# Fourier channel mixing rewritten: four images in a row, columns held twice, each layer as four 64x64 parts of the array

## The chip, the cores and the metric

The kernel runs on one core of a Trainium2 chip. The metric is the device time of one execution in microseconds (us), the median of the runs. The core has five engines with a queue each: TensorE (PE; its weight loads are listed apart as PEld), VectorE (DVE), ScalarE (ACT), GpSimd (POOL) and SyncE (SP). A suffix q (SPq, ACTq) is an engine's sequencer, which issues DMAs, waits and branches.

## The reference, cut to what matters

The model is a chain of attention, Fourier mixing, attention, routed experts and retention on an input of 4 images, 48x48 tokens, 192 channels. The stage at hand is in the second block:

```python
def _L1_conv_ref(x, w1, b1, w2, b2, Wb, bb):
    bias = x @ Wb.T + bb
    xb = x.reshape(Bsz, Hh, Ww, nb, bs)                       # 4 blocks of 48 channels
    xf = jnp.fft.rfftn(xb, axes=(1, 2), norm='ortho')
    y = jnp.einsum('bhwnd,ndk->bhwnk', xf, w1) + b1           # complex, block by block
    y = _crelu(y)                                             # relu of the real and the imaginary part
    y = jnp.einsum('bhwnd,ndk->bhwnk', y, w2) + b2
    out = jnp.fft.irfftn(y, s=(Hh, Ww), axes=(1, 2), norm='ortho')
    return out.reshape(Bsz, Hh, Ww, Cc) + bias
```

The two-dimensional transform is split: `fourier_front` does the rows (48 positions to 25 complex values), `fourier_mix` the columns, both complex layers and the columns back, `fourier_back` the rows back. `fourier_mix` is what changes. The experts (`run_experts`) compute `gelu(x @ w1 + b1) @ w2 + b2` for 8 experts.

## The kernel before

All stages stand one behind the other in one program. Each allocates its tiles and semaphores, opens a block with one hand-written queue per engine, and ends with a barrier of all engines. Nothing of a stage starts before that barrier, so a stage's length adds to the total as a whole. No scheduler orders anything: each queue runs in the order of the code, and semaphores counted (`full`: a bank is written; `free`: a bank is evacuated) tie them.

`fourier_mix` works on one image at a time, in a hardware loop (`Fori`, a counted loop with a branch back at its end) over the 4 images on SP, PE and ACT. An image is 48 rows, real and imaginary (96 partitions), by 25 columns by 192 channels in float32. The channels are handled as two halves of 96 (two blocks of 48 each).

1. SP (L1031) loads the image into the one tile `columns`, two DMAs of 900 KB. It waits for `full` at the image's first use number (L1029), that is until PE has done everything of the image before.
2. PE (L1052) transforms the columns: 5 matmuls of 96 columns each fill a PSUM bank (one of four accumulators of 512 float32 per partition), 10 banks in all. ACT copies each into `layer0` (L1100).
3. PE does the two layers (L1064, L1066, L1068): for each of 10 groups per layer one matmul with the real weights over 480 columns and two with the imaginary ones (one negated) over 240 columns. The weights are 96x96 with two 48x48 blocks on the diagonal and zeros elsewhere. ACT evacuates each bank in two pieces with the bias, and in the first layer relu (L1109).
4. PE transposes the result, 50 transposes in 13 banks (L1076); ACT copies them into `turned` (L1116).
5. PE transforms back, 10 matmuls of 480 columns (L1083); ACT copies into `back` (L1123) and issues two DMAs of 900 KB to `mixed` (L1127).

PE takes a bank when the use four before it is evacuated (`take`, L1043). VectorE only negates the weights once (L1091). A float32 matmul shows as two records of PEld and two of PE in the trace, a transpose as one.

`run_experts` runs its 8 experts two to a pass of a loop that is opened by `hinted` (L29), which marks the branch back for the instruction fetch on each engine (L2188, L2219, L2231).

## Time and profile before

| what | us |
|---|---|
| median of 3 runs | 7612.12 |
| the runs | 7607.83 to 7624.61 |
| profiled execution, own time | 7621.83 |
| profiled execution, span | 7620.3 |
| `fourier_mix`, first matmul to last copy | 2758.02 to 3030.56 |
| PE busy in the span | 6538.7 (86%) |
| mean granted TensorE clock | 0.904 |

The profile gives for each stretch the busy time of every engine, the clock that TensorE was granted (1.00 is its 2.4 GHz level, 0.50 its 1.2 GHz level) and what the DMA engines moved. The timeline gives instructions in order of time, equal ones merged: the start, the time covered, the engine, the line, the operation, what is written and read, the size of the array part used (rows*columns), shape, count, and the idle time before with what ended it. A matmul's record is longer than the array is occupied by it, since records overlap; so the pace is read from the distance between starts.

### The profile page before, as it was taken

To read this page: it belongs to the slowest core of one execution; us is meant where nothing else is said; L and a number is where in the kernel's file an instruction comes from. 1 tells how busy PE (TensorE), PEld (TensorE's weight loads), DVE (VectorE), ACT (ScalarE), POOL (GpSimd) and SP (SyncE) were. 2 spreads that over 40 slices of the span, in tenths; PEclk is the share of its full clock that TensorE was granted. 3 is DMA by queue.
4 is the path that set the end of the run, shared out by engine and by line. 5 is a ranking of instruction groups with operands and counts; after the bars stand their busy time and mean duration, and the time that the engine had idled before them with its cause. 6 is when DMAs were issued, how large, how long until landed. Compare 5 with 4: busy or idle time off the path is not lost. (4 is left out here: it accounts for less than half of the span.)

```text
span 7620.3 us, 232590 instructions
## 1 busy us (share of the span) xinstructions
PE 6538.7 (86%) x87259; PEld 4110.7 (54%) x87259; DVE 4712.1 (62%) x7690; ACT 3159.9 (41%) x5333; POOL 2306.5 (30%) x2558
## 2 busy tenths in 40 slices
PE   6699999999997677499999995299779999999977
PEld 4255555555554554266767674176445555555546
DVE  6788888888884410222323236211779999999976
ACT  2067666766665134022222221021444444444432
POOL 0011111111111000000000000300349999999961
PEclk8699999999998688699999995599889999999986
DMA  3211111111112422401010003222741111111123
GB/s 117 77 36 38 36 38 34 38 37 38 38 38 56 136 68 53 142 1 29 1 29 1 19 14 118 69 68 49 225 146 36 37 38 36 37 38 36 37 69 100
DMA packets 424933, 428.90 MB, mean 56 GB/s; under 512 B 77729, under 2 KB 397961, under 8 KB 419051
## 3 DMA queue, kind: packets, MB, share of 16 engines
q1 hardware_dynamic: 342123, 339.77, 16.0%
q0 software_dynamic: 62528, 59.16, 3.3%
q10 hardware_dynamic: 19712, 21.53, 0.9%
q8 instruction: 460, 7.54, 0.4%
q14 instruction: 110, 0.90, 0.0%
HBM read 253.62 MB, written 166.55 MB: 55 GB/s over the span
## 5 line engine op out<-in xcount | busy, mean ns | idle before, releaser
L633 DVE TENSOR_REDUCE softmax_part_max<-softmax_ring 128x1 f32<-128x512 f32 (+1 forms) x2880 | 1680.5, 633 | 333.8 <-PE softmax_ring L541 276.4
L2517 POOL TENSOR_TENSOR retention_decayed<-retention_third,retention_decay_table 128x384 f32<-128x384 f32 x1728 | 1690.6, 1005 | 104.3 <-ACT retention_third L2539 100.0
L2498 DVE TENSOR_TENSOR retention_decayed<-retention_scores,retention_decay_table 128x768 f32<-128x768 f32 x1728 | 1654.7, 958 | 90.4 <-PE retention_scores L2459 58.3
L673 ACT ACTIVATE softmax_probs<-softmax_scores 128x768 f32<-128x768 f32 x1728 | 1392.1, 810 | 678.8 <-PE softmax_scores L563 605.8
L541 PE MATMUL softmax_ring<-softmax_k_next,softmax_q_next 96*32 96x512 bf16 (+1 forms) x11520 | 1116.9, 377 | 182.8 <-issue 74.6
L2459 PE MATMUL retention_scores<-retention_q_half,retention_k_piece 96*32 96x384 bf16 x20736 | 1184.7, 325 | 36.1 <-DMA retention_v_piece<-ret_v 29.1
L2539 ACT COPY retention_third<-retention_scores 128x384 f32<-128x384 f32 x1728 | 826.6, 478 | 892.4 <-PE retention_scores L2459 892.4
L2471 PE MATMUL retention_sums<-retention_decayed,retention_v_piece 128*32 128x288 f32 x13824 | 1182.5, 407 | 3.4 <-POOL retention_decayed L2517 0.6
L2459 PEld LDWEIGHTS retention_scores<-retention_q_half,retention_k_piece 96*32 96x32 bf16 x20736 | 625.5, 95 | 520.1 <-DVE retention_decayed L2498 41.7
L574 PE MATMUL softmax_sums<-softmax_probs,softmax_v_piece 128*32 128x192 f32 x13824 | 883.4, 330 | 13.3 <-issue 12.6
L563 PE MATMUL softmax_scores<-softmax_q_third,softmax_k_piece 99*32 99x384 bf16 x13824 | 886.7, 332 | 3.1 <-DMA softmax_v_piece<-rope_v 1.8
L505 POOL DMA_DIRECT2D rope_out<-softmax_result x384 | 195.4, 510 | 1727.1 <-ACT softmax_result L662 1676.0
L541 PEld LDWEIGHTS softmax_ring<-softmax_k_next,softmax_q_next 96*32 96x32 bf16 x11520 | 306.9, 95 | 681.1 <-DVE softmax_part_max L633 437.5
L574 PEld LDWEIGHTS softmax_sums<-softmax_probs,softmax_v_piece 128*32 128x32 f32 x13824 | 425.3, 112 | 208.9 <-issue 29.0
L1493 DVE TENSOR_REDUCE wide_top<-wide_scores 128x1 f32<-128x2304 f32 x72 | 184.1, 2558 | 504.8 <-PE wide_scores L1387 504.8
L2471 PEld LDWEIGHTS retention_sums<-retention_decayed,retention_v_piece 128*32 128x32 f32 x13824 | 344.0, 109 | 260.5 <-issue 179.7
L563 PEld LDWEIGHTS softmax_scores<-softmax_q_third,softmax_k_piece 99*32 99x32 bf16 x13824 | 363.1, 97 | 178.4 <-ACT softmax_probs L673 25.8
L1417 PE MATMUL wide_valued_bank<-wide_v,wide_probs_t 128*128 128x192 f32 x2592 | 440.5, 329 | 2.2 <-ACT wide_probs_t L1481 2.2
L1417 PEld LDWEIGHTS wide_valued_bank<-wide_v,wide_probs_t 128*128 128x128 f32 x2592 | 419.2, 190 | 25.6 <-issue 22.5
L1354 POOL TENSOR_TENSOR wide_residual<-wide_residual,wide_bo 96x2304 f32<-96x2304 f32 x8 | 40.2, 5043 | 1056.2 <-DMA wide_residual<-x 1056.2
L1381 PE MATMUL wide_scores<-wide_qk_t 128*128 128x512 f32 (+1 forms) x720 | 329.4, 559 | 2.3 <-ACT wide_v L1465 2.3
L1472 ACT ACTIVATE wide_probs<-wide_scores,wide_shift 128x2304 f32<-128x2304 f32 x72 | 157.0, 2180 | 414.5 <-DVE wide_shift L1495 414.5
(303 smaller groups left out, 6685.6 us busy)
## 6 DMA issues: line engine op xcount, KB each, us to landing
ret_v<-ret_proj_values SPq DMA_DIRECT2D x8, 1728.0 KB, 8.7
retention_v_piece<-ret_v SPq DMA_DIRECT2D x144, 96.0 KB
softmax_q_third<-rope_q SPq DMA_DIRECT2D x192, 54.0 KB
softmax_q_next<-rope_q POOLq DMA_DIRECT2D x64, 162.0 KB, 3.9
softmax_k_piece<-rope_k SPq DMA_DIRECT2D x192, 54.0 KB
softmax_k_next<-rope_k POOLq DMA_DIRECT2D x64, 162.0 KB, 6.2
ret_q<-ret_proj_parts SPq DMA_DIRECT2D x48, 216.0 KB, 2.8
ret_k<-ret_proj_parts SPq DMA_DIRECT2D x48, 216.0 KB, 3.1
```

What stands on the lines that cost most here:

```text
L541: last = nc.tensor.matmul(ring[m % 2][32 * g:32 * g + 32, 0:width], q_next[i][:, rows:rows + 32], k_next[i][:, at:at + width], start=True, ...
L563: last = nc.tensor.matmul(scores[n % 2][32 * g:32 * g + 32, c, 0:QC], k_piece[t // PT][:, at:at + 32], q_third[third][:, c * QC:(c + 1) * ...
L574: last = nc.tensor.matmul(sums[third % 2][32 * g:32 * g + 32, 0:VC], v_piece[t // PT][:, t % PT, :], probs[n % 4][:, g * VC:(g + 1) * VC], ...
L633: nc.vector.reduce_max(part_max[:, j, c:c + 1], ring[m % 2][:, 0:CHUNKS[c][1]], axis=X)\
L673: nc.scalar.activation(probs[n % 4][:, :].rearrange("p (c q) -> p c q", c=2), scores[n % 2][:, :, 0:QC], ACT.Exp, scale=scale).then_inc(ex ...
L1381: nc.tensor.matmul(scores[:, at:at + width], qk_t[:, 0, 0, i * P:(i + 1) * P], qk_t[:, 1, 0, at:at + width], start=True, stop=False)
L1417: last = nc.tensor.matmul(valued_bank[:, 0:C], probs_t[:, t * P:(t + 1) * P], v[:, t, :], start=(t == 0), stop=(t == TILES - 1))
L2459: last = nc.tensor.matmul(scores[n % 2][32 * g:32 * g + 32, c, 0:QC], k_piece[t // PT][:, at:at + 32], q_half[half][:, c * QC:(c + 1) * QC ...
L2471: last = nc.tensor.matmul(sums[half][32 * g:32 * g + 32, 0:VC], v_piece[t // PT][:, t % PT, :], weights[n % 4][:, g * VC:(g + 1) * VC], st ...
L2498: nc.vector.tensor_tensor(weights[n % 4][:, 0:2 * QC].rearrange("p (c q) -> p c q", c=2), scores[n % 2][:, 0:2, 0:QC], table[:, table_at(n ...
L2517: nc.gpsimd.tensor_tensor(weights[n % 4][:, 2 * QC:HALF], third[n % 3][:, :], table[:, at:at + QC], ALU.mult)\
L2539: nc.scalar.copy(third[n % 3][:, :], scores[n % 2][:, 2, 0:QC]).then_inc(third_copied, 1)
```

## The change

`fourier_mix` is written anew.

- The loop over the images is written out on PE, ACT and DVE (no branch). `columns` exists twice; SP loads images 0 and 1 ahead, image 0 before the tables, and image b+2 as soon as the column transform of image b is issued (`FIRST_LAYER` uses).
- All 8 PSUM banks are used instead of 4. Bank uses are numbered through; even ones are evacuated by ACT (`act_free`), odd ones by DVE (`dve_free`).
- The two 48-channel blocks of a half stand at partitions 0 to 47 and 64 to 111 (`ROW` = 64). A column-transform matmul makes 48 output rows instead of 96, so there are 100 in place of 50 per image.
- A layer handles 10, 10 and 5 values of k at a time, real results in one bank and imaginary ones in another. Each matmul is one block, 48 by 64: (rows 0, columns 0), (64, 64) for the real part and (0, 64), (64, 0) for the imaginary one. The imaginary result thus comes out with its blocks exchanged, and DVE writes them back exchanged (L1172). Eight matmuls of 480 columns serve a group of 10.
- Transposes take 112 columns in place of 96; gaps of 16 are skipped when they are copied. The partitions between the blocks and the weights' borders are cleared by POOL once.
- `hinted` goes, and the loops of `run_experts` become plain `Fori`.

```diff
-def hinted(nc, eng, start, end):
-
-    return nc.Fori(start, end, engines=bass.OrderedEngineSet([eng.engine]), hint_back_edge=True)
...
+    ROW = 64
+    WIDE = ROW + BS
     H2 = 2 * H
...
+    BANKS = 8
+    LOADS = [(half, k, 5) for half in range(2) for k in range(0, KW, 5)]
+    GROUPS = [(half, k, min(10, KW - k)) for half in range(2) for k in range(0, KW, 10)]
+    TURNS = [((k, 0), (k, 1), (k + 1, 0), (k + 1, 1)) for k in range(0, KW - 1, 2)] + [((KW - 1, 0),), ((KW - 1, 1),)]
...
+            load(0)
+            for to, of in [(identity[:, :], ident), (forward[:, :], column_dft), (inverse[:, :], column_inverse)]:
+                sp.dma_start(to, of).then_inc(tables_in, 16)
+            sp.wait_ge(cleared, 3)
+            for n in range(2):
+                block_n = slice(n * BS, (n + 1) * BS)
+                sp.dma_start(weights[row(n), :, :, :, 0:BS].rearrange("p i r f c -> p (i r f) c"),
+                             mix[block_n, :, :, :, block_n].rearrange("p i r f c -> p (i r f) c")).then_inc(consts_in, 16)
+                sp.dma_start(biases[row(n), :, :, :], mix_bias[block_n, :, :, :]).then_inc(consts_in, 16)
+                sp.dma_start(crossed[row(1 - n), :, :], mix_bias[block_n, :, 1, :]).then_inc(consts_in, 16)
+            load(1)
+            for b in range(images - 2):
+
+                sp.wait_ge(full, b * USES + FIRST_LAYER)
+                load(b + 2)
...
+            def take(b, n):
+
+                if b or n >= BANKS:
+                    if (b * USES + n) % 2 == 0:
+                        pe.wait_ge(act_free, by_act(b, n - BANKS))
+                    else:
+                        pe.wait_ge(dve_free, by_dve(b, n - BANKS))
+                return bank_of(b, n)
...
+            def products(out, of, sign, i, part, half, source, k0, count, start):
+
+                z = source[:, half, k0:k0 + count, part, :]
+                for at, to in of:
+                    use = minus[row(at), i, half, :] if sign < 0 else weights[row(at), i, sign, half, :]
+                    last = nc.tensor.matmul(out[to * ROW:to * ROW + ROW, 0:count * H], use, z[row(at), :, :], start=start, stop=not start)
+                return last
+
+            pe.wait_ge(tables_in, 48)
+            STRAIGHT, SWAPPED = [(0, 0), (1, 1)], [(0, 1), (1, 0)]
+            for b in range(images):
+                pe.wait_ge(columns_in[b % 2], (b // 2 + 1) * 32)
...
+                        real, imag = take(b, first + 2 * g), take(b, first + 2 * g + 1)
+                        products(real, STRAIGHT, 0, i, 0, half, layer[i], k0, count, True)
+                        products(imag, SWAPPED, 1, i, 0, half, layer[i], k0, count, True)
+                        products(real, STRAIGHT, -1, i, 1, half, layer[i], k0, count, False).then_inc(full, 1)
+                        products(imag, SWAPPED, 0, i, 1, half, layer[i], k0, count, False).then_inc(full, 1)
...
-            with hinted(nc, eng, 0, E // 2 - 1) as pair:
+            with eng.Fori(0, E // 2 - 1) as pair:
```

On PE, one image ends and the next begins like this before (`fft_mix_turned` to `fft_mix_bank` is the transform back; the branch closes the loop):

```order
L1043 REGISTER_ALU
L1083 MATMUL fft_mix_bank<-fft_mix_turned,fft_mix_inverse 96x480
L1037 REGISTER_ALU
L1037 COMPARE_AND_BRANCH
L999 UNCONDITIONAL_BRANCH
```

and now, from the last rows of the second layer of one image to the column transform of the next:

```order
L1095 MATMUL fft_mix_bank<-fft_mix_layer,fft_mix_minus 64x240 x2
L1095 MATMUL fft_mix_bank<-fft_mix_layer,fft_mix_weights 64x240 x2
L1125 MATMUL fft_mix_bank<-fft_mix_identity,fft_mix_layer 96x112 x50
L1132 MATMUL fft_mix_bank<-fft_mix_turned,fft_mix_inverse 96x480 x10
L1107 MATMUL fft_mix_bank<-fft_mix_forward,fft_mix_columns 48x96 x100
```

The branch is gone, and the column transform has twice the matmuls with half the output rows.

On PE, from the end of the column transform into the layers, one group before:

```order
L1052 MATMUL fft_mix_bank<-fft_mix_forward,fft_mix_columns 96x96 x5
L1043 REGISTER_ALU
L1064 MATMUL fft_mix_bank<-fft_mix_layer,fft_mix_weights 96x480
L1066 MATMUL fft_mix_bank<-fft_mix_layer,fft_mix_weights 96x5x48
L1068 MATMUL fft_mix_bank<-fft_mix_layer,fft_mix_weights 96x5x48
```

and now the three groups of one half (4, 2 and 2 matmuls each; neighbours of one name are merged, so that two groups share the row of 6):

```order
L1095 MATMUL fft_mix_bank<-fft_mix_layer,fft_mix_weights 64x480 x4
L1095 MATMUL fft_mix_bank<-fft_mix_layer,fft_mix_minus 64x480 x2
L1095 MATMUL fft_mix_bank<-fft_mix_layer,fft_mix_weights 64x480 x6
L1095 MATMUL fft_mix_bank<-fft_mix_layer,fft_mix_minus 64x480 x2
L1095 MATMUL fft_mix_bank<-fft_mix_layer,fft_mix_weights 64x480 x2
L1095 MATMUL fft_mix_bank<-fft_mix_layer,fft_mix_weights 64x240 x4
L1095 MATMUL fft_mix_bank<-fft_mix_layer,fft_mix_minus 64x240 x2
L1095 MATMUL fft_mix_bank<-fft_mix_layer,fft_mix_weights 64x240 x2
```

Three matmuls on the whole array became eight, each on a quarter of it; each row of 4 goes round the four parts once.

On SP, the start of the stage before and now (tiles and the tensors in memory that they are loaded from):

```order
L1026 DMA fft_mix_identity<-table_ident 128x128
L1026 DMA fft_mix_forward<-table_column_dft 96x96
L1026 DMA fft_mix_inverse<-table_column_inverse 96x96
L1026 DMA fft_mix_weights<-fourier_mix 96x2x384
L1026 DMA fft_mix_biases<-fourier_mix_bias 96x8
```

```order
L1046 DMA fft_mix_columns<-spectrum 48x4800 x2
L1050 DMA fft_mix_identity<-table_ident 128x128
L1050 DMA fft_mix_forward<-table_column_dft 96x96
L1050 DMA fft_mix_inverse<-table_column_inverse 96x96
L1054 DMA fft_mix_weights<-fourier_mix 48x8x48
L1056 DMA fft_mix_biases<-fourier_mix_bias 48x8
```

The first image has moved ahead of the tables, and the weights come in two parts with shorter runs.

## Rows read from the trace of the kernel before

**Rows 1.** Stretches of the stage: length, busy us (records) per engine, granted clock, DMA share, GB/s.

```profile
2741.00:2758.00 17.00, 0.00 (x0) 0.00 (x0) 0.35 (x1) 0.00 (x0) 0.00 (x0) 0.50 0.70 134
2758.00:2770.00 12.00, 11.98 (x101) 11.84 (x102) 0.00 (x0) 5.11 (x10) 0.00 (x0) 0.72 0.00 1
2780.00:2816.00 36.00, 35.10 (x153) 20.67 (x151) 0.00 (x0) 21.93 (x53) 0.00 (x0) 1.00 0.00 1
2816.00:2829.00 13.00, 0.00 (x0) 0.00 (x0) 0.00 (x0) 0.00 (x0) 0.00 (x0) 0.63 1.00 263
6000.00:6400.00 400.00, 397.70 (x8060) 224.79 (x8056) 385.53 (x404) 199.05 (x425) 393.87 (x404) 1.00 0.13 37
```

**Rows 2.** Timeline of the first image: loads, column transform, layers, transposes, transform back, next image.

```profile
2741.47 0.37 SPq L1026 DMA_DIRECT2D fft_mix_identity<-table_ident  x1
...
2744.51 0.83 SPq L1031 DMA_DIRECT2D fft_mix_columns<-spectrum  x2
...
2758.02 11.83 PE L1052 MATMUL fft_mix_bank<-fft_mix_forward,fft_mix_columns 96*96 96x96 f32 x100 [21.52 <-DMA fft_mix_columns<-spectrum]
...
2763.16 0.56 ACT L1100 COPY fft_mix_layer<-fft_mix_bank 96x480 f32<-96x480 f32 x1 [1.04 <-PE fft_mix_bank L1052]
2764.76 0.55 ACT L1100 COPY fft_mix_layer<-fft_mix_bank 96x480 f32<-96x480 f32 x1 [1.04 <-PE fft_mix_bank L1052]
...
2767.34 0.56 ACT L1100 COPY fft_mix_layer<-fft_mix_bank 96x480 f32<-96x480 f32 x1 [0.29 <-PE fft_mix_bank L1052]
2768.19 0.56 ACT L1100 COPY fft_mix_layer<-fft_mix_bank 96x480 f32<-96x480 f32 x1 [0.29 <-PE fft_mix_bank L1052]
...
2769.69 0.97 PE L1064 MATMUL fft_mix_bank<-fft_mix_layer,fft_mix_weights 96*96 96x480 f32 x2
...
2801.99 4.82 PE L1076 MATMUL fft_mix_bank<-fft_mix_identity,fft_mix_layer 96*96 96x96 f32 x50
...
2806.82 8.29 PE L1083 MATMUL fft_mix_bank<-fft_mix_turned,fft_mix_inverse 96*96 96x480 f32 x20
...
2815.28 0.82 SPq L1031 DMA_DIRECT2D fft_mix_columns<-spectrum  x2
2815.86 0.84 ACTq L1127 DMA_DIRECT2D mixed<-fft_mix_back  x2
...
2829.15 12.09 PE L1052 MATMUL fft_mix_bank<-fft_mix_forward,fft_mix_columns 96*96 96x96 f32 x100 [14.04 <-DMA fft_mix_columns<-spectrum]
```

**Rows 3.** Timeline: the last copy of the stage, its store, the next stage's first DMA.

```profile
3030.01 0.55 ACT L1123 COPY fft_mix_back<-fft_mix_bank 96x480 f32<-96x480 f32 x1 [0.25 <-PE fft_mix_bank L1083]
3030.72 0.80 ACTq L1127 DMA_DIRECT2D mixed<-fft_mix_back  x2
3041.66 0.30 SPq L1157 DMA_DIRECT2D fft_back_row_inverse<-table_row_inverse  x1
```

**Rows 4.** Timeline of the experts: row parts (64*128), then full matmuls; 120-column transposes.

```profile
5014.21 0.57 PE L2249 MATMUL experts_tr_bank<-experts_identity,experts_tokens 120*128 120x120 f32 x4
...
5014.62 3.39 PE L2263 MATMUL experts_hid_bank<-experts_turned,experts_w 128*128 128x480 f32 x8
...
5017.95 1.88 PE L2267 MATMUL experts_hid_bank<-experts_turned,experts_w_over 64*128 64x480 f32 x8
...
5019.76 4.16 PE L2278 MATMUL experts_out_bank<-experts_w,experts_hidden 128*120 128x192 f32 x24
```

**Rows 5.** PE's timeline in the retention heads (column parts), across a pass of its loop.

```profile
5735.72 0.69 PE L2471 MATMUL retention_sums<-retention_decayed,retention_v_piece 128*32 128x288 f32 x8
5736.21 0.70 PE L2459 MATMUL retention_scores<-retention_q_half,retention_k_piece 96*32 96x384 bf16 x12
5736.70 0.69 PE L2471 MATMUL retention_sums<-retention_decayed,retention_v_piece 128*32 128x288 f32 x8
5737.52 0.67 PE L2459 MATMUL retention_scores<-retention_q_half,retention_k_piece 96*32 96x384 bf16 x12
```

**Rows 6.** PE's timeline in the softmax heads, short column parts, and across its loop.

```profile
2202.90 0.50 PE L574 MATMUL softmax_sums<-softmax_probs,softmax_v_piece 128*32 128x192 f32 x8
2203.23 0.39 PE L541 MATMUL softmax_ring<-softmax_k_next,softmax_q_next 96*32 96x512 bf16 x4
...
2205.19 0.50 PE L574 MATMUL softmax_sums<-softmax_probs,softmax_v_piece 128*32 128x192 f32 x8
2205.62 0.40 PE L541 MATMUL softmax_ring<-softmax_k_next,softmax_q_next 96*32 96x512 bf16 x4
...
507.03 0.40 PE L541 MATMUL softmax_ring<-softmax_k_next,softmax_q_next 96*32 96x512 bf16 x4 [2.69 <-issue]
```

**Rows 7.** Groups by line, form kept apart: VectorE reading a bank.

```profile
L2330 DVE COPY experts_turned<-experts_tr_bank 128x480 f32<-128x480 f32 x48 | 31.2, 649 | 112.5 <-PE experts_tr_bank L2249 112.1
...
L1509 DVE TENSOR_SCALAR wide_heads<-wide_valued_bank,wide_inverse 128x192 f32<-128x192 f32 x72 | 30.1, 418 | 5.6
...
L971 DVE COPY fft_front_rows_out<-fft_front_dft_bank 100x384 f32<-100x384 f32 x48 | 26.7, 557 | 55.1 <-PE fft_front_dft_bank L918 55.1
```

More of the change, by code:

```diff
@@ L1007, in fourier_mix @@
+        columns = [sb(f"columns{i}", [H2, KW, C], F32) for i in range(2)]
+        layer = [sb(f"layer{i}", [WIDE, 2, KW, 2, H], F32) for i in range(3)]
         turned = sb("turned", [H2, KW, C], F32)
         back = sb("back", [H2, KW, C], F32)
-        bank = [ps(f"bank{i}", [P, 512], F32) for i in range(4)]
-        consts_in, columns_in = sem("consts_in"), sem("columns_in")
-        full, free, stored, negated = sem("full"), sem("free"), sem("stored"), sem("negated")
+        bank = [ps(f"bank{i}", [P, 512], F32) for i in range(BANKS)]
@@ new lines, in loaded_part, with turned_part @@
+        def loaded_part(n, block_n):
+            half, k0, count = LOADS[n]
+            return layer[0][row(block_n), half, k0:k0 + count, :, :].rearrange("p k r h -> p (k r h)")
+        def turned_part(t):
+            k, half = TURNS[t][0]
+            count = len(TURNS[t])
+            if count == 1:
+                return turned[:, k, half * HC:(half + 1) * HC].rearrange("p (j n c) -> p j n c", j=1, n=2)
+            return turned[:, k:k + 2, :].rearrange("p k (f n c) -> p (k f) n c", f=2, n=2)
```

227 lines of the change are left out of this document (130 added, 97 removed).

## The prediction

> **What bounds the kernel now.** The stages follow each other behind barriers, so I need only the stage that changes and, for the loops of the experts, that stage. I read the stretches of the column-mixing stage first [rows 1]. The reader is to see three states of one image: PE busy at a clock of 0.72 on average after a stretch at 0.50, PE busy at 1.00 in the layers (35.1 of 36.0 us), and 13 us in which no engine computes while the DMA engines are busy all the time. The timeline gives the borders [rows 2]: image 0 starts at 2758.02, its layers at 2769.69, its transposes at 2801.99, its transform back at 2806.82, image 1 at 2829.15. So an image is 11.7 + 32.3 + 4.8 + 8.1 us of PE work and some 14 us of waiting for the next image's load, which is issued only at 2815.28, when PE has finished. From the first matmul to the end of the last copy the stage takes 3030.56 - 2758.02 = 272.5 us [rows 2, 3]. PE bounds it wherever there is data: ACT, the only engine that evacuates, is busy 21.9 us of the 36 [rows 1]; only in the transposes do its copies set the pace.
>
> **The layers (the largest term).** A 480-column pass of a float32 matmul takes 0.402 us of the array: eight 64-row records took 5019.76 - 5017.95 = 1.81 us, which is four of them in a row plus 0.20 us for changing the array's division there and back [rows 4]. That they were four in a row and not eight is the evidence that two row parts run at once, each into its own bank over all columns. For column parts, eight float32 records of 288 columns start 0.49 us before the next group (5735.72 to 5736.21) [rows 5]; at 0.402 us for 480 columns one of them is 0.241 us, eight in a row would be 1.93 us, so four ran at once. Rows and columns divided together are not in this trace. I take the product, four quarters at once. Then a group of 8 matmuls (16 passes) takes 4 x 0.402 = 1.61 us and one of 240 columns 0.81 us. A half is 2 x 1.61 + 0.81 = 4.03 us, two halves of two layers 16.1 us, against 32.3 now. Gain: 16.2 us per image, 64.8 in all. Bounds: 16.1 (four at once) and 64.4 (one by one); I take the first since both directions taken alone reach their full factor.
>
> **The wait for the load** goes. The next image is loaded behind the one before: a load takes 2758.02 - 2744.51 = 13.5 us, and load and store together 13.9 us at the border of two images [rows 2], against some 38 us per image. Three waits of 14.0 to 14.5 us lie between four images; I count 3 x 14.2 = 42.6 us. With them goes the slow clock. The granted clock is 0.50 when the wait ends [rows 1], and the ACT copies that follow the banks stand 1.60 us apart at first and 0.85 later, five matmuls each [rows 2]. Ten banks at 0.85 would be 8.5 us; they took 11.7. So 3.2 us per image, and for three of the four images it goes, since PE no longer pauses: 9.6 us. Retention, divided into narrow parts too, holds 1.00 over 400 us [rows 1].
>
> **The column transform** doubles its matmuls: 200 records instead of 100, of 96 columns each, on half the array's columns. Now one record takes 0.085 us. If two halves run at once it stays at 8.5 us; if not, 17.0. The nearest rows are the softmax sums, eight float32 records of 192 columns in 0.33 to 0.43 us [rows 6], 0.041 to 0.054 each with a weight load apiece, where four at once would be 0.040. I take 0.045, that is 9.0 us, 0.5 more than now, 2.0 in all.
>
> **Transposes and transform back.** 50 transposes of 112 columns: 4 of 120 columns take 5014.62 - 5014.21 = 0.41 us [rows 4], so 112 take 0.096 each, 4.8 us; the same as now, when ACT's copies set the pace. The transform back is the same 20 records, 8.05 us. Changing the division of the array three times per image costs 3 x 0.1 to 3 x 0.2 us [rows 4]; I take 0.4 us per image, 1.6 in all.
>
> **Evacuation** has to hide beside PE. In a half-layer of 4.03 us DVE makes four passes of 480 and two of 240. Copies of 480 and 384 columns from a bank take 0.649 and 0.557 us, which is 0.96 ns a column, and a 192-wide instruction with a scalar operand takes 0.418 [rows 7]; widened by that rate it is 0.70 us for 480 and 0.46 for 240. The half-layer costs DVE between 3.4 us (as copies) and 3.7: hidden, by a margin of 0.3 us. If such an instruction took 0.80 us (0.56 for 240), DVE would need 4.3 us, each of the 16 half-layers would last 0.3 us longer, 5 us in all. ACT has one 480-wide instruction per group, some 0.6 us of 1.61. In the column transform each engine has ten copies of 0.56 (ACT, [rows 2]) or 0.65 us, at most 6.5 us of 9.0. Eight banks let PE run four groups ahead.
>
> **The start.** The load is issued at 2741.47 instead of 2744.51, but PE also waits for three tables of 136 KB that now queue behind it; at the 134 GB/s of that stretch [rows 1] 1.0 us. So PE starts near 2755.9, a gain of 2.1 us. Weights in short runs and the biases arrive later; ACT and DVE wait for them, and eight banks at 1.60 us cover 12 us. POOL's clearing lies beside the load. The store at the end is the same: from the last copy to the next stage's first DMA 11 us [rows 3].
>
> **The experts' loops** lose their mark on the branch: two branches back are taken on PE. The retention loop has no mark, and across its branch the distance is 0.82 instead of 0.49 us [rows 5]; the softmax loop has none and PE idles 2.69 us [rows 6]. A pass of the experts' loop has by its code 480 PE records, retention's 720, softmax's some 2,450. So the near row is retention: 0 to 0.7 us, and 5.4 at the other end. I take 0, since the experts' matmuls are longer and PE has them queued ahead of the branch.
>
> The Trainium skill, "Runtime: NRT & Kernel Launch", section "Instruction fetch mechanics", says that fetching runs ahead in order and that a branch costs a fetch when its target is outside what the engine holds. The rows agree as far as they go (0.33 us against 2.69). By that rule the code written out costs nothing and the unmarked short loop costs nothing, so the sum stays.
>
> **Sum.** One image: 9.0 + 16.1 + 4.8 + 8.05 + 0.4 = 38.35 us; four are 153.4, with 3.2 for the slow clock of the first 156.6. PE ends at 2755.9 + 156.6 = 2912.5 instead of 3029.8. That is 117.3 us less (64.8 + 42.6 + 9.6 + 2.1 - 2.0 - 1.6 = 115.5 from the parts, the rest is in the borders). The profiled execution took 7621.83 us, 0.13% over the median of 7612.12; it would be 7504.5, and the median 7495.
>
> **Rivals.**
> - *Only two of the four quarters at once.* The two straight matmuls write the two halves of one bank from different row parts; no row shows that. If they, and the two exchanged ones, exclude each other, a group takes 8 x 0.402 us and the layers stay at 32.2 us. The gain shrinks by 4 x 16.1 = 64.4 to 53: 7559. For it: the missing row. Against it: full factors in either direction [rows 4, 5]. The Trainium skill, "TensorEngine Tiling (Array Packing)", section "Gotcha 1: PSUM Pressure", states just this, that different row tiles cannot use the same bank at the same time; by it the result would be this rival's. The rows of before only have row parts in different banks.
> - *The column halves don't overlap:* 17.0 instead of 9.0 us per image, 7527.
> - *Fetching cannot keep up* with some 1,000 instructions per image written out: at 2.69 us [rows 6] for each of some 16 blocks up to 43 us, 7538. Against it: retention issues as densely.
> - *Slower than before.* If nothing overlaps in the quarters, the layers take 64.4 us and the transform 17.0, an image 94.7, the stage ends 108 us later: 7720. The point from which it decides: an image of 67.7 us breaks even, so layers of 45 us, an overlap under 1.4 instead of 4.
> - *The change doesn't do what it says:* evacuation on DVE bounds the layers. Priced above at 5 us; it would have to double to matter.
>
> **How the numbers follow.** The forecast with its small bounds (start, softmax's 0.041 to 0.054, DVE, the loops' 0 to 5.4) spans 7484 to 7514: 0.74. Column halves apart 0.06, fetching 0.06, two at once 0.08, slower 0.03, something within the noise 0.01, better than all 0.02. The range 7482 to 7540 takes in the first three. A measurement of this kernel can tell about 0.2% from no change. Faster by more: 0.96; within 0.2%: 0.01; slower: 0.03.
>
> **What would show it.** In the profile after: image starts 38 us apart with no wait for the load between them; eight 480-column matmuls per 1.6 us (3.2 would be the rival); the clock at 1.00 from the middle of image 0 on; PE idle under 1 us per image for DVE; no idle PE at the branch of the experts' loop. A start-to-start of 54 us per image would make the prediction wrong.

## The result and the profile after

| | before | changed |
|---|---|---|
| median of 4 runs each, us | 7613.76 (7607.83 to 7624.61) | 7510.99 (7509.17 to 7527.41) |
| ratio, with its 95% interval | 1 | 0.9866 (0.9853 to 0.9878) |
| profiled execution: time, span, us | 7621.83, 7620.3 | 7509.17, 7507.6 |
| column-mixing stage: its first instruction to the next stage's, us | 300.2 | 191.4 |
| PE, first matmul of image 0, 1, 2, 3, then last copy ends (us from the stage's first instruction) | 16.6, 87.7, 159.4, 231.3, 289.1 | 13.7, 59.9, 97.6, 141.7, 180.1 |

The change makes the kernel 1.3% faster. The forecast was 7495 in a range of 7482 to 7540: inside the range, but the point lies 16 us too low. The stage came out 108.8 us shorter, where the forecast had 117.3. By its interval the whole kernel gained 93 to 112 us. The untouched stages differ by a few us from execution to execution (the first one took 280.6 us and 286.3), so from here on stages are compared and not spans.

The frame of the stage, in the timeline of the changed kernel (start, length, engine with q for its queue, line, operation, out<-in):

```profile
2747.48 0.80 SPq L1046 DMA_DIRECT2D fft_mix_columns<-spectrum  x2
...
2926.93 0.65 DVE L1184 COPY fft_mix_back<-fft_mix_bank 96x480 f32<-96x480 f32 x1 [0.95 <-PE fft_mix_bank L1132]
2927.68 0.80 ACTq L1220 DMA_DIRECT2D mixed<-fft_mix_back  x2
2938.91 0.30 SPq L1250 DMA_DIRECT2D fft_back_row_inverse<-table_row_inverse  x1
```

PE in the same timeline. In brackets stands the idle time ahead of a row and what ended it; "issue" means that the engine waited for nothing that the profile shows:

```profile
2761.15 9.07 PE L1107 MATMUL fft_mix_bank<-fft_mix_forward,fft_mix_columns 96*48 96x96 f32 x147 [18.64 <-DMA fft_mix_inverse<-table_column_inverse]
2772.51 3.36 PE L1107 MATMUL fft_mix_bank<-fft_mix_forward,fft_mix_columns 96*48 96x96 f32 x53 [2.28 <-issue]
2775.80 1.88 PE L1095 MATMUL fft_mix_bank<-fft_mix_layer,fft_mix_weights 48*64 48x480 f32 x8
...
2794.42 5.00 PE L1125 MATMUL fft_mix_bank<-fft_mix_identity,fft_mix_layer 112*96 112x112 f32 x50
2799.26 8.22 PE L1132 MATMUL fft_mix_bank<-fft_mix_turned,fft_mix_inverse 96*96 96x480 f32 x20
2807.40 8.46 PE L1107 MATMUL fft_mix_bank<-fft_mix_forward,fft_mix_columns 96*48 96x96 f32 x200
2815.79 1.03 PE L1095 MATMUL fft_mix_bank<-fft_mix_layer,fft_mix_weights 48*64 48x480 f32 x8
...
2832.07 5.00 PE L1125 MATMUL fft_mix_bank<-fft_mix_identity,fft_mix_layer 112*96 112x112 f32 x50
2836.90 8.21 PE L1132 MATMUL fft_mix_bank<-fft_mix_turned,fft_mix_inverse 96*96 96x480 f32 x20
2845.05 8.45 PE L1107 MATMUL fft_mix_bank<-fft_mix_forward,fft_mix_columns 96*48 96x96 f32 x198
2856.97 0.55 PE L1107 MATMUL fft_mix_bank<-fft_mix_forward,fft_mix_columns 96*48 96x96 f32 x2 [3.47 <-issue]
2857.45 1.88 PE L1095 MATMUL fft_mix_bank<-fft_mix_layer,fft_mix_weights 48*64 48x480 f32 x8
...
2876.20 5.00 PE L1125 MATMUL fft_mix_bank<-fft_mix_identity,fft_mix_layer 112*96 112x112 f32 x50
...
2889.18 8.46 PE L1107 MATMUL fft_mix_bank<-fft_mix_forward,fft_mix_columns 96*48 96x96 f32 x200
```

Read it by the starts. An undisturbed image is image 1: 8.39 us of column transform (2807.40 to 2815.79), 16.28 of layers (to 2832.07), 4.83 of transposes, 8.15 of transform back, 37.65 in all, against 71.1 from image 0 to image 1 before [rows 2]. No wait for a load is left. Images 0 and 2 are longer, 46.25 and 44.13 us, and the rows show where: PE stands still for 2.28 us ahead of the last 53 records of image 0's transform, and for 3.47 us ahead of the last two of image 2's. Nobody in the program is waited for.

The stretches (length, busy us and records of PE, PEld, DVE, ACT, POOL, granted clock, DMA share, GB/s), which answer to [rows 1]:

```profile
2769.00:2776.00 7.00, 4.72 (x86) 4.26 (x86) 2.71 (x5) 2.63 (x5) 0.00 (x0) 0.84 0.21 49
2776.00:2780.00 4.00, 4.00 (x24) 1.24 (x25) 1.84 (x3) 0.66 (x1) 0.00 (x0) 0.50 0.98 158
...
2816.00:2832.00 16.00, 16.00 (x192) 7.04 (x184) 14.62 (x23) 6.84 (x12) 0.00 (x0) 1.00 0.67 132
2850.00:2857.00 7.00, 3.53 (x85) 3.33 (x80) 2.62 (x4) 2.76 (x5) 0.00 (x0) 0.90 0.50 154
2857.00:2861.00 4.00, 4.00 (x22) 1.49 (x26) 1.31 (x2) 0.04 (x1) 0.00 (x0) 0.50 0.01 4
```

In the layers of image 1 PE is never idle, at the clock of 1.00, and DVE is busy 14.6 of 16 us beside it. After each of these two pauses the granted clock is 0.50, the lower of its two levels, in the stretch shown, and the layers of images 0 and 2 take 18.62 and 18.75 us instead of 16.28.

### The profile page after: what moved, and what is told of

It reads as the page before. It is cut to its first block and busy times, and to the rows that moved or that the text cites. A ratio compares the mean times of both kernels' runs of the same rounds, so it can differ in the third digit from the quotient of the medians.

```text
span 7507.6 us, 233537 instructions
## 1 busy us (share of the span) xinstructions
PE 6455.2 (86%) x87947; PEld 4044.6 (54%) x87947; DVE 4825.5 (64%) x7874; ACT 3107.2 (41%) x5177; POOL 2309.5 (31%) x2562
```

## The experiments

### What the waits and the clock were worth alone

The kernel before with the columns held twice; layers and evacuation untouched:

```diff
-        columns = sb("columns", [H2, KW, C], F32)
+        columns = [sb(f"columns{i}", [H2, KW, C], F32) for i in range(2)]
...
+            load(0)
+            load(1)
+            for b in range(images - 2):
+                sp.wait_ge(full, b * USES + GROUPS)
+                load(b + 2)
...
-            with pe.Fori(0, images) as b:
+            for b in range(images):
```

> The kernel before with the columns held twice, the loads ahead, and PE's and SP's images of the column mixing written out; layers, parts of the array and evacuation as before. By the sum of the prediction this is the waits for the load (42.6 us) and the clock (9.6 us) alone: stage shorter by 52 us, kernel 7562 us, ratio 0.9931; image starts 57 us apart (8.5 + 32.3 + 4.8 + 8.1 = 53.7 to 57). The rival, that most of what the changed kernel gained lies in the overlap of load and store and not in the layers, would give over 70 us here.

Measured: 7563.72 us, ratio 0.9931 (0.9915 to 0.9948), stage 249.5 us, 50.7 less than before. PE's timeline, image 1 and image 2:

```profile
2813.75 8.71 PE L1056 MATMUL fft_mix_bank<-fft_mix_forward,fft_mix_columns 96*96 96x96 f32 x100 [0.74 <-ACT fft_mix_back L1127]
...
2868.45 8.71 PE L1056 MATMUL fft_mix_bank<-fft_mix_forward,fft_mix_columns 96*96 96x96 f32 x100 [0.74 <-ACT fft_mix_back L1127]
```

An image is 54.7 us, and the transform takes 8.55 us at the full clock. The two terms of 42.6 and 9.6 us hold (50.7 against 52.2). The changed kernel gains 249.5 - 191.4 = 58.1 us beyond this one. Most of that is the layers, 32.30 us an image here and 16.28 there, 64.1 us in four images; PE is the engine that sets their pace in both. The earlier start gives 2.7 us (first matmul after 13.7 us instead of 16.4). Against these stand the pauses, priced below. The rest is small, such as PE's wait of 0.74 us for a bank in each image, seen in the brackets above. No run has the eight banks and the second evacuating engine without the quarters, so these small parts aren't told apart.

### The experts' marks

The changed kernel with the marks put back:

```diff
-            with eng.Fori(0, E // 2 - 1) as pair:
+            with hinted(nc, eng, 0, E // 2 - 1) as pair:
```

(likewise in the loops of SP and POOL.)

> The changed kernel with the marks on the experts' three loops put back, nothing else. The prediction took their removal at 0 us, with 5.4 at the other end. Theory A (PE has its matmuls queued ahead of the branch): the experts' stage stays within 1 us of the changed kernel's (425.9 us from its first instruction to the next stage's), kernel within 0.1% of it, ratio to before 0.985 to 0.988. Rival (each unmarked branch back costs a fetch, as the softmax loop's 2.69 us): the experts' stage gets 5.4 us shorter.

The experts' stage took 425.4 us with the marks, 425.9 without. The changed kernel's variants below, all without marks, lie between 424.0 and 425.6. The median was 7529.95 us, and the ratio, 0.9888 (0.9868 to 0.9908), lies just above the expected 0.985 to 0.988. It is no evidence on the marks: the retention stage, whose code is the same, took 1748.9 us from its first instruction to its last store in the profiled execution, and 1732.7 in the changed kernel's. PE's timeline of the changed kernel across the branch, which lies at 5024.6:

```profile
5022.72 4.16 PE L2371 MATMUL experts_out_bank<-experts_w,experts_hidden 128*120 128x192 f32 x24
5026.72 0.57 PE L2342 MATMUL experts_tr_bank<-experts_identity,experts_tokens 120*128 120x120 f32 x4
```

The 24 matmuls take 4.00 us from start to start, as long as an expert earlier (4922.70 to 4926.70), where no branch lies, and PE isn't idle. No block of instructions for PE (queue q8, read below) arrives between 4919 and 5142, so this branch fetched nothing, and the run tells nothing of a loop that does fetch at its branch. In the column-mixing stage the same kernel had pauses as well, in other amounts: 1.85 us in image 0, 0.74 in image 2, 1.93 in image 3.

### Where the pauses come from

Three guesses: PE's next block of instructions is held up by the transfers that are in flight (A), PE uses up its instructions faster than they come, whatever else goes on (B), or the pauses are evacuation in disguise (C). First, no transfer beside a column transform:

```diff
-            load(1)
-            for b in range(images - 2):
+            for b in range(images - 1):
                 sp.wait_ge(full, b * USES + FIRST_LAYER)
-                load(b + 2)
+                load(b + 1)
...
+                if b:
+                    store(b - 1)
                 for i, first in enumerate((FIRST_LAYER, SECOND_LAYER)):
```

(`store` is ACT's store of an image with its two waits, which stood at the end of the image's work.)

> The changed kernel, with the load of the next image issued after the column transform of the image (image 1's too) and the store of an image issued by ACT only after its copies of the next image's column transform: no load or store is in flight during any column transform. In the changed kernel PE pauses 3.5 to 3.7 us twice, in the column transforms of images 0 and 2, with nothing that it waits for, and each time the granted clock falls after it; these two transforms take 14.65 and 12.40 us instead of 8.39, the layers behind them 18.62 and 18.75 instead of 16.28. Theory A (PE's next 16 KB of instructions lies behind the packets of the load or store, 19,200 bytes each): both pauses go, image 2 takes 37.65 us like images 1 and 3, image 0 its transform at a clock of 0.50 to 1.00 (8.5 to 11.7 us) and layers near 16.3; stage shorter by 9 to 12 us, kernel about 7500. Theory B (PE works through its instructions faster than they are fetched, whatever else is in flight): both pauses stay, kernel 7509 to 7513. Theory C (the pauses are evacuation or banks): they stay too, and a copy ends when they end.

Measured: 7490.25 us, ratio 0.9833 (0.9819 to 0.9847), stage 178.2 us, 13.2 under the changed kernel, which is more than the 9 to 12 expected. All pauses are gone: each image after the first takes 37.65 us, image 0's layers 16.28. Its transform at a rising clock takes 10.12 us. B and C fall, as the instructions, the copies and their rate are the same. Long-rowed loads and stores still run in this version, beside the layers, and PE doesn't pause there. The second try keeps the transfers where they are and makes them of shorter rows:

```diff
                 for r in range(2):
-                    sp.dma_start(columns[b % 2][r * H:(r + 1) * H, :, :], spectrum[b, :, r, :, :]).then_inc(columns_in[b % 2], 16)
+                    for k in range(0, KW, 5):
+                        sp.dma_start(columns[b % 2][r * H:(r + 1) * H, k:k + 5, :], spectrum[b, :, r, k:k + 5, :]).then_inc(columns_in[b % 2], 16)
```

(the stores on ACT likewise.)

> The changed kernel with each load and each store of an image in ten transfers (rows of 3,840 bytes) instead of two (rows of 19,200); nothing else is moved, so that loads and stores are in flight at the same places. Theory A (a fetch of instructions stands behind long packets): the pauses of 3.5 us shrink below 1 us, stage shorter by 8 to 12 us, kernel about 7500. If it is the amount of data in flight and not the length of a packet, the pauses stay. Theory B (code is fetched too slowly anyway): they stay, kernel within 3 us of the changed one, plus the cost of more issues (SP and ACT issue ten instead of two, some 0.5 us each; ACT's stand ahead of its copies of the next image, up to 4 us per image).

Measured: 7515.8 us, ratio 0.986 (0.9845 to 0.9875), stage 196.7 us. The expected price of ACT's issues was too low. Timeline of image 1:

```profile
2799.72 6.81 PE L1108 MATMUL fft_mix_bank<-fft_mix_forward,fft_mix_columns 96*48 96x96 f32 x160
...
2800.57 7.74 ACTq L1222 DMA_DIRECT2D mixed<-fft_mix_back  x10
...
2808.35 5.69 ACT L1201 COPY fft_mix_layer<-fft_mix_bank 48x480 f32<-48x480 f32 x10 [8.78 <-DVE fft_mix_layer L1166]
...
2809.52 3.44 PE L1108 MATMUL fft_mix_bank<-fft_mix_forward,fft_mix_columns 96*48 96x96 f32 x40 [3.00 <-ACT fft_mix_layer L1201]
```

ACT issues for 7.74 us before it copies, and PE fills its eight banks (160 records) and waits: these pauses have a name in the brackets. Image 0, ahead of which no store is issued, had none: transform 10.19 us, layers 16.28. No pause marked "issue" is left in this stage. So the issues went to SP, where no copies queue behind them:

> The changed kernel with loads and stores at the places where they are now, each in ten transfers of 3,840-byte rows, and all issued by SP, so that ACT issues nothing. With ten transfers and ACT issuing the stores, image 0's pause was gone, but ACT issued for 7.74 us before its copies and PE waited for it in images 1 to 3. Theory A1 (a fetch of instructions stands behind long packets): no pause here in any image, images 1 to 3 take 37.65 us each, kernel 7495 to 7503. Theory A2 (what matters is how much data is in flight beside the fetch): a pause of 3 to 4 us in at least one image. No evidence for A1 if the fetches happen to fall outside the transfers: where each fetch lies is read beside it.

And as its partner the same with long rows, so that the two differ only in the length of the rows, and so in ten transfers or two for the same bytes:

> The changed kernel with SP issuing the stores instead of ACT, loads and stores in two transfers of 19,200-byte rows as in the changed kernel. It differs from the version without pauses only in the length of the packets (that one had ten transfers of 3,840-byte rows at the same places and from the same queue; stage 176.5 us). Theory A1 (a fetch of PE's instructions is held up by long packets): pauses of 1 to 4 us in two or three images again, stage 184 to 192 us. Rival (ACT as the issuer of the stores caused them): no pause, stage 176 to 179 us.

| | rows, bytes | stage, us | pauses of PE, us |
|---|---|---|---|
| changed kernel | 19,200 | 191.4 | 2.28, 3.47 |
| the same once more | 19,200 | 190.5 | 2.64, 1.30, 2.03 |
| the same with the marks back | 19,200 | 186.8 | 1.85, 0.74, 1.93 |
| long rows, SP issues | 19,200 | 184.9 | 1.88, 1.83 |
| short rows, SP issues | 3,840 | 176.5 | none |
| no transfer beside a transform | 19,200 | 178.2 | none |

The short rows' version ran 7501.2 us, ratio 0.9847 (0.9829 to 0.9865), the long rows' 7514.5, ratio 0.9865 (0.9848 to 0.9881); these intervals overlap, the stages and the traces are what tells the two apart. Of the 8.4 us between their stages 1.8 are no pause: with ten pieces PE's first matmul comes 11.7 us after the first transfer, with two 13.5. PE's timeline with long rows, its two idle places:

```profile
2763.05 2.39 PE L1114 MATMUL fft_mix_bank<-fft_mix_forward,fft_mix_columns 96*48 96x96 f32 x53 [1.88 <-issue]
2842.55 0.37 PE L1114 MATMUL fft_mix_bank<-fft_mix_forward,fft_mix_columns 96*48 96x96 f32 x2 [1.83 <-issue]
```

These are the places of the changed kernel's pauses: ahead of the last 53 records in image 0, of the last two in image 2. In every profile of this code with long rows PE pauses ahead of these two instructions, with another length each time. That is a border in the code. Two of the profiles have a third pause, in the layers of image 3; this is the one of the changed kernel's second profile:

```profile
2890.40 0.62 PE L1095 MATMUL fft_mix_bank<-fft_mix_layer,fft_mix_weights 48*64 48x480 f32 x2 [2.03 <-issue]
```

The DMA queues also show packets of the kind `instruction`, blocks of code on their way to an engine. The pauses of PE go with those of queue q8. Narrow windows tell when such a packet runs (queue, packets, MB, share of the 16 engines). The changed kernel in image 2, whose transform starts at 2845.05 and whose pause ends at 2856.97, over 2846 to 2854.7 and over 2854.7 to 2855.7:

```profile
q10 hardware_dynamic: 116, 1.79, 83.6%
```

```profile
q10 hardware_dynamic: 9, 0.06, 16.4%
q8 instruction: 1, 0.02, 6.0%
```

And the kernel with short rows and SP issuing, at the same place: PE, and the queues over 2828.2 to 2829.3:

```profile
2823.74 8.46 PE L1116 MATMUL fft_mix_bank<-fft_mix_forward,fft_mix_columns 96*48 96x96 f32 x200
```

```profile
q1 hardware_dynamic: 61, 0.18, 83.8%
q8 instruction: 1, 0.02, 5.6%
```

In the changed kernel the block runs at 2854.7 to 2855.7, after PE has stopped, and PE goes on 1.3 us after the block's end. All 15 pauses of more than 0.5 us marked "issue" in this stage, in the seven profiles with long rows beside the transforms, end like that, 1.2 to 1.5 us after the end of such a packet. So they are waits for instructions. And what the row length changes is when the block starts, not how long it runs (0.9 to 1.6 us in all of them):

| beside the transform | block starts, us after the transform of image 0 | of image 2 |
|---|---|---|
| long rows (four profiles of the same PE code) | 8.4 to 9.3 | 7.0 to 9.7 |
| short rows (ACT issues; SP issues) | 3.3; 2.9 | 3.7; 4.6 |
| no transfer | 1.3 | 2.6 |

PE needs the block's instructions some 8 to 9 us after the transform starts, so the block, with its run and the 1.3 us behind it, has to start some 2.5 us ahead of that. With long rows it comes too late, with short ones in time, though there is as much data in flight: 303 GB/s over 2831 to 2834 in the short rows' image 2. A packet takes 83.6% x 16 x 8.7 us / 116 = 1.0 us in the changed kernel and 83.8% x 16 x 1.1 us / 61 = 0.24 us here, small ones included.

So A holds, and it is the length of the packets, not the amount in flight. Long rows don't always stop PE: in image 1 of the changed kernel a store runs at 168 GB/s over 2807 to 2815, the block starts 2.2 us after the transform, and there is no pause. That a late block was queued behind long packets is the reading that fits; the moment at which it is asked for isn't in the trace, and that is left open.

### Does the order around the quarters matter?

The same matmuls, but both products of a quarter in a row, and in the column transform five matmuls on one half of the columns, then five on the other:

```diff
-                        products(real, STRAIGHT, 0, i, 0, half, layer[i], k0, count, True)
-                        products(imag, SWAPPED, 1, i, 0, half, layer[i], k0, count, True)
...
+                        for to, quarters, signs in ((real, STRAIGHT, (0, -1)), (imag, SWAPPED, (1, 0))):
+                            for quarter in quarters:
+                                for part in range(2):
...
-                    for k in range(count):
-                        for block_n in range(2):
+                    for block_n in range(2):
+                        for k in range(count):
```

> The changed kernel with the same matmuls issued in another order: in the layers both products of a quarter behind each other, quarter by quarter, instead of once around the four; in the column transform five matmuls on one half of the array's columns, then five on the other, instead of by turns. Theory in order: matmuls start in program order, and one holds up what stands behind it while its part is busy. Then two quarters at most run at once in the layers: a group of eight takes 3.2 us instead of 1.6, the two layers 32.2 us instead of 16.3, and the column transform 14 to 17 us instead of 8.4; an image is 22 to 25 us longer, the kernel 7597 to 7610. Rival (each part of the array has a queue of its own, so that the order doesn't matter): layers 16.3 and transform 8.4 us, kernel 7510.

It ran 7516.27 us, a single time. The theory in it fell, and its rival holds for the layers alone. PE's timeline of image 1:

```profile
2802.28 11.26 PE L1107 MATMUL fft_mix_bank<-fft_mix_forward,fft_mix_columns 96*48 96x96 f32 x200
2813.46 1.06 PE L1095 MATMUL fft_mix_bank<-fft_mix_layer,fft_mix_weights 48*64 48x480 f32 x8
2814.32 0.57 PE L1095 MATMUL fft_mix_bank<-fft_mix_layer,fft_mix_minus 48*64 48x480 f32 x2
```

The layers took 16.43 us instead of 16.28, and the transform 11.19 instead of 8.39, where 16.8 would be no overlap. In the program a quarter's `minus` records are the third and fourth, yet eight `weights` records of all four quarters start before them. So a record waits for its part of the array, and those of other parts pass it. How many? Runs of 20 records on one half (ten matmuls, each two records):

> The changed kernel with the column transform's matmuls in longer runs on one half of the array's columns: ten on the first half (into two banks), then ten on the second, where the changed kernel takes the halves by turns. Runs of five took 11.2 us an image where by turns took 8.39 (and 16.8 would be no overlap). Theory D (PE starts matmuls out of program order where their parts of the array are free, but only so far ahead): runs of ten overlap less, 13 to 15.5 us an image. Rival (the loss of runs of five lies only at the borders of runs, by the changes of part): runs of ten lose less, 9.5 to 11 us. The layers are untouched, 16.3 us.

```profile
2851.82 14.12 PE L1109 MATMUL fft_mix_bank<-fft_mix_forward,fft_mix_columns 96*48 96x96 f32 x200
2865.88 1.04 PE L1095 MATMUL fft_mix_bank<-fft_mix_layer,fft_mix_weights 48*64 48x480 f32 x8
```

14.05 us in images 2 and 3, which have no pause. (The single time, 7590.05 us, holds 1788.3 us of retention stage, 55.6 more than the changed kernel's; the stage itself took 202.8.) Both fit one number, with x the records that can stand before a busy part: 16.8 x (1 - x/10) = 11.2 and 16.8 x (1 - x/20) = 14.05 both give x = 3.3. By it, runs of eight must hurt the layers:

> The changed kernel with the layers' matmuls in longer runs on one quarter of the array: both products of two groups (four matmuls, eight records of the trace), then the next quarter. The column transform with runs of 10 and 20 records on one half took 11.2 and 14.05 us an image instead of 8.39, and 16.8 would be no overlap: both fit a part that may fall about 3.3 records behind before it holds up the other (16.8 x (1 - 3.3/10) = 11.3, 16.8 x (1 - 3.3/20) = 14.0). Runs of 4 records in the layers fit too (16.43 us, nothing lost). Theory Q (some three records can stand before a part of the array): a run of 8 records of 480 columns holds up the next for (8 - 3.3) x 0.402 = 1.9 us instead of 0.8, the two layers take 30 to 38 us instead of 16.3, the kernel 7565 to 7600. Rival (four full quarters whatever the order): 16.3 to 19 us, kernel 7510 to 7520.

```profile
2837.20 1.01 PE L1095 MATMUL fft_mix_bank<-fft_mix_layer,fft_mix_weights 48*64 48x480 f32 x2
2838.05 0.96 PE L1095 MATMUL fft_mix_bank<-fft_mix_layer,fft_mix_minus 48*64 48x480 f32 x2
2838.86 1.02 PE L1095 MATMUL fft_mix_bank<-fft_mix_layer,fft_mix_weights 48*64 48x480 f32 x4
2839.66 1.02 PE L1095 MATMUL fft_mix_bank<-fft_mix_layer,fft_mix_minus 48*64 48x480 f32 x4
...
2874.45 5.00 PE L1131 MATMUL fft_mix_bank<-fft_mix_identity,fft_mix_layer 112*96 112x112 f32 x50
```

37.25 us of layers (2837.20 to 2874.45), the kernel 7593.72, a single time. The formula above gives 64.4 x (1 - 3.3/8) = 37.8 us, where 64.4 is one quarter at a time. The rows show it happening: four records alone on the first quarter, 0.4 us each, and only with its fifth, when three are left behind it, does the second quarter join (x4 instead of x2 in the same time).

### A version that is faster

The transfers moved out of the transforms, as above, and image 0 in pieces:

```diff
-    LOADS = [(half, k, 5) for half in range(2) for k in range(0, KW, 5)]
+    LOADS = [(half, k, 5) for k in range(0, KW, 5) for half in range(2)]
...
+            for k in range(0, KW, 5):
+                for r in range(2):
+                    sp.dma_start(columns[0][r * H:(r + 1) * H, k:k + 5, :], spectrum[0, :, r, k:k + 5, :]).then_inc(piece_in[k // 5], 16)
...
+                    if b == 0 and half == 0:
+                        pe.wait_ge(piece_in[k0 // 5], 32)
```

(ACT and DVE wait for the weights only before the layers; the first 12 frequencies of the last image are stored while the rest is computed.)

> No load or store during a column transform after the first, as in the second kernel here, and also: the first image comes in five pieces of five frequencies, the column transform goes through the frequencies piece by piece (both halves of a piece), ACT and DVE no longer wait for the weights before it, and of the last image's result the first 12 frequencies are stored while the rest is computed. Stage against the moved one: first matmul some 7 to 9 us after the first transfer instead of 14, the transform then paced by the load to 15 to 17 us instead of 24; the end 2 to 4 us earlier. Expected 8 to 12 us under the moved kernel, 7479 to 7484 us; if the half-idle PE is granted the slow clock into the layers, 2.5 us of it are lost. Rival (first pieces are slowed by the tables and the stage is bound by the layers' weights, which come last): no gain, 7490.

It ran 7490.48 us, ratio 0.9834 (0.9818 to 0.9851), stage 170.8. The stage is 7.4 us under the moved kernel's, but the forecast for the whole kernel was missed: its median is the same as the moved kernel's 7490.25. Beside the changed kernel on one chip:

> The version with the transfers moved out of the column transforms, the first image in pieces and the last store in two, once more and beside the changed kernel. Expected: no pause, stage 170 to 172 us, 16 to 22 us under the changed kernel's, ratio to before 0.982 to 0.985; if its lower time was chance, its stage is within 5 us of the changed kernel's.

> The changed kernel once more, unaltered, beside the two versions of it that are quicker, on one chip. Its stage took 191.4 us in the first profile and 186.8 us in the one with the marks put back (the same code in this stage): the pauses for instructions fall in different places. Expected: pauses of 1 to 5 us in two or three of the four images, stage 186 to 193 us, ratio to before 0.985 to 0.989.

Changed kernel 7512.98 us, ratio 0.9862 (0.9842 to 0.9882), stage 190.5; this version 7488.02 us, ratio 0.9834 (0.9818 to 0.9849), stage 166.4. The stage is 24.1 us shorter, more than the expected 16 to 22, the medians lie 25 apart, and the intervals only just overlap. What the pieces add to the moved transfers is seen in the stage alone. Its timeline and its first stretches:

```profile
2747.86 0.35 SPq L1051 DMA_DIRECT2D fft_mix_forward<-table_column_dft  x1
...
2748.25 4.61 SPq L1054 DMA_DIRECT2D fft_mix_columns<-spectrum  x10
2751.91 10.81 PE L1116 MATMUL fft_mix_bank<-fft_mix_forward,fft_mix_columns 96*48 96x96 f32 x200 [9.00 <-DMA fft_mix_columns<-spectrum]
...
2764.63 1.04 PE L1100 MATMUL fft_mix_bank<-fft_mix_layer,fft_mix_weights 48*64 48x480 f32 x8 [1.91 <-DVE fft_mix_layer L1172]
```

```profile
2752.00:2764.00 12.00, 10.73 (x200) 10.52 (x200) 6.45 (x10) 5.53 (x10) 0.86 (x1) 0.80 0.65 143
2765.00:2781.00 16.00, 16.00 (x193) 8.41 (x186) 13.55 (x22) 6.67 (x11) 0.00 (x0) 1.00 0.54 95
```

PE starts 4.1 us after the first transfer instead of 13.7 (7 to 9 were expected) and is through the transform after 16.8 instead of 28.3. In the first profile of this version the layers of image 0 took 19.58 us, in this one 16.28; the other images took 37.65 us both times.

## The prediction against the runs, step by step

**The layers** were right: 16.28 us for 16.1, four quarters at once. The rival of two at once would have shown 32. The Trainium skill, "TensorEngine Tiling (Array Packing)", section "Gotcha 1: PSUM Pressure", was that rival's ground. Here the two straight products write the two halves of one bank from different row parts, and nothing was lost, so the measurement decides against the rule for this form. Rows and columns divided together give the product of the two factors.

**Waits and clock** were right: 52.2 us, 50.7 by the kernel that has them alone.

**The column transform** was 0.6 us too dear (8.39 for 9.0): 8.39 + 16.28 + 4.83 + 8.15 = 37.65, for a forecast of 38.35. Of the 0.4 us for changing the array's division at most 0.3 show, since the layers, transposes and transform back took 0.31 us more than their own terms (29.26 for 28.95). That is the lower of the prediction's two values, three changes at 0.1 us.

**Evacuation** hides, as said. DVE's instructions took 716 and 466 ns, for 0.70 and 0.46 us:

```profile
L1172 DVE TENSOR_SCALAR fft_mix_layer<-fft_mix_bank,fft_mix_crossed 48x480 f32<-48x480 f32 x64 | 45.8, 716 | 9.8 <-PE fft_mix_bank L1095 7.5
...
L1172 DVE TENSOR_SCALAR fft_mix_layer<-fft_mix_bank,fft_mix_crossed 48x240 f32<-48x240 f32 x32 | 14.9, 466 | 0.8
```

**The start** came 0.7 us earlier than said (13.7 us after the first transfer, for 14.4), and the slow clock cost image 0's transform 1.7 us, for 3.2 (10.12 against 8.39, in the kernel without pauses).

**The step that failed** is "the code written out costs nothing", and with it the sentence "so the sum stays". The sum leaned on a row in which instructions were issued as densely while transfers of 37 GB/s ran beside them [rows 1]; here they ran at 168 and 180 GB/s beside the transforms of images 0 and 2, in long packets. That row was also no evidence on fetching: in its 400 us not one packet of queue q8 arrives, so the retention loop went round without fetching code for PE. In this stage 15 arrive. What was priced at nothing is PE's wait for a block of instructions that comes late. The rival "fetching cannot keep up" had the mechanism, at 43 us and a chance of 0.06, but its condition wrong: the rate of the code alone doesn't do it, since without long packets beside it the same code never stops. Measured cost: image 0's transform 14.65 - 10.12 = 4.5 us, its layers 18.62 - 16.28 = 2.3, image 2's 4.0 and 2.5, in all 13.3 us. The Trainium skill, "Runtime: NRT & Kernel Launch", section "Instruction fetch mechanics", calls the cost of a border between blocks mostly hidden; the trace agrees for the kernels with no or short-rowed transfers and disagrees at some of the borders where rows of 19,200 bytes are in flight (0.74 to 3.47 us a time). The pauses themselves are 2.28 and 3.47 us, less than half of the 13.3. The rest is slow clock, most of it behind the pauses; in image 0 about 1.0 us lies ahead of the pause, where the first 147 records took 8.8 us and in the kernel without pauses 7.8.

**The books.** 13.3 us too little for the pauses, less 2.8 for four images at 37.65, less 1.5 for the clock of image 0, less 0.7 for the start, and 0.2 more at the end (11.3 us from the last copy's end to the next stage, where it was 11.1) give 8.5; measured 117.3 - 108.8 = 8.5. The rest of the 16 us between forecast and median isn't in the stage. The forecast took 9.5 us off for the step from the profiled execution to the median, where the changed kernel's profiled execution lies 1.8 under its median, and the untouched stages happened to be 3.9 shorter: 8.5 + 11.3 - 3.9 = 15.9. That the median still lies within the small bounds, 7484 to 7514, is luck: they had no term for pauses.

**The experts' loops** cost nothing without their marks, as taken.

**What was to be seen:** image starts 38 us apart without waits (37.65, where no pause lies in between), eight 480-column matmuls per 1.6 us, no PE idle for DVE in the layers, none at the experts' branch: all there. The clock at 1.00 from the middle of image 0 on: not so, it was at 0.50 again at the start of the layers of images 0 and 2, right behind the pauses.

## What to carry to other kernels

Transfers of the same bytes do not cost the same: beside a stretch in which PE works through many short instructions, keep long-rowed transfers away or break their rows up, and let an engine issue them that has no other work queued behind them. When a matmul uses a part of the array, the others are free for other matmuls, in both directions at once; change the part after at most four records, that is two float32 matmuls, the longest run on a quarter that cost next to nothing here (0.15 of 16.28 us). A term priced "nothing" on the strength of one row should name what ran beside that row, and show that the row has the thing at all (here: arriving blocks of instructions).

## What the runs showed that was not expected

- *Matmuls of different parts of the array pass each other.* Some 3.3 records can stand before a busy part before it holds up the others: runs of 4 records lose 0.15 of 16.3 us, runs of 10 cost 11.2 for 8.4 us, of 20 14.05, and runs of 8 long ones 37.25 for 16.3. The Trainium skill, "TensorE: Matmul & The Clock Gate", section "Step-by-step: what each phase is for", says that matmuls stay in program order. Their starts here don't, as soon as they use different parts.
- *A pause of PE for instructions* lies at fixed places of the code, has a length of 0.74 to 3.47 us from one execution of this PE code to the next, shows as "issue", and ends 1.2 to 1.5 us after an instruction block has landed. Not each slowed what came behind: after 0.74 and 1.30 us in image 2 and after 1.85 and 1.88 in image 0 the layers took 16.28 us, after 1.83 in image 2 17.98.
- *Ten stores issued in a row take longer than their number says.* ACT needed 7.74 us for ten, 0.77 each, in which it copied nothing, and 0.80 for two. It isn't ACT: SP took 8.21 us for the ten stores of an image, and 4.52 for the ten loads of the first.
- *The retention stage* of the same code took 1732.7 to 1788.3 us in these profiles (first instruction to last store); a single time of this kernel can mislead by 0.7%.
